# A product moved to GpSimd: the route's row multiplies the gate instead of the hidden tile in 16 units of an expert FFN

## The reference, cut to what matters

```python
masked_w = softmax over the 8 largest of x @ gate_w.T, 0 elsewhere   # tokens x 32
g = einsum('th,eih->tei', x, w_gate_proj)
u = einsum('th,eih->tei', x, w_up_proj)
h = silu(g) * u * masked_w[:, :, None]
out = einsum('tei,ehi->th', h, w_down_proj)
```

## Time and profile before

| | us |
|---|---|
| median of 3 runs | 777.99 |
| lowest, highest | 775.37, 778.99 |
| the profiled execution | 776.41 |
| its span | 774.6 |
| PE, DVE, ACT, POOL busy | 687.4, 548.6, 416.4, 247.1 |

### The profile page before, as it was taken

The page is one execution under the profiler, slowest core; times in us unless marked ns, Lnnn a source line. Parts: engine busy times, 40 slices in busy tenths (PEclk is TensorE's granted clock), DMA queues, the critical chain, the costliest instruction groups (busy, mean ns, idle before and its releaser), DMA issues.

```text
span 774.6 us, 10077 instructions
## 1 busy us (share of the span) xinstructions
PE 687.4 (89%) x3424; PEld 532.3 (69%) x3424; DVE 548.6 (71%) x1061; ACT 416.4 (54%) x814; POOL 247.1 (32%) x243
## 2 busy tenths in 40 slices
PE   5176746999998999999899999988899898999997
PEld 1154533455556788888788999977798776888885
DVE  5999997799998666565477666776766466544454
ACT  5575615646424544454667777766677445334342
POOL 0100001000053244454356565644465243212231
PEclk9598786999999999999999999999999999999999
DMA  7347753566664174443111111110112233433240
GB/s 238 118 151 236 231 166 113 149 209 199 202 165 149 51 205 137 142 164 120 45 41 46 37 43 41 41 42 15 42 55 76 82 123 111 127 118 100 84 137 27
DMA packets 43987, 88.67 MB, mean 114 GB/s; under 512 B 6136, under 2 KB 8448, under 8 KB 43936
## 3 DMA queue, kind: packets, MB, share of 16 engines
q1 hardware_dynamic: 43936, 88.04, 36.2%
HBM read 82.44 MB, written 5.57 MB: 114 GB/s over the span
## 4 chain that ended last, share of the span: by engine, by line
PE 57%; DVE 28%; issue 8%; ACT 6%; DMA 0%; DVEq 0%; POOL 0%; SPq 0%; ACTq 0%
PE bank L89 17%; PE bank L90 17%; PE bank L91 17%; DVE state L1115 9%; DVE read_out L1125 3%; PE bank L654 2%; DVE drive L1106 2%; ACT probs L967 2%; DVE bank L1268 1%; DVE u_sb L1028 1%; DVE scores L1388 1%; DVE stats L1035 1%; DVE x_norm L1048 1%; PE bank L485 1%; DVE head_out_lo L1017 1%
## 5 line engine op out<-in xcount | busy, mean ns | idle before, releaser
L1461 POOL TENSOR_TENSOR w_lo<-w_raw,w_hi 128x768 fp32r<-128x768 f32 (+1 forms) x90 | 152.1, 1690 | 290.9 <-ACT w_hi L737 289.6
L89 PE MATMUL bank<-xt_hi,w_hi 128*128 128x512 f32 x336 | 134.6, 401 | 0.0
L90 PE MATMUL bank<-xt_lo,w_hi 128*128 128x512 f32 x336 | 132.5, 394 | 0.0
L91 PE MATMUL bank<-xt_hi,w_lo 128*128 128x512 f32 x336 | 132.5, 394 | 0.0
L737 ACT ACTIVATE w_hi<-w_raw 128x768 fp32r<-128x768 f32 (+1 forms) x90 | 69.0, 766 | 87.4 <-PE bank L91 84.3
L1017 DVE TENSOR_TENSOR hidden_lo<-bank,hidden_hi 128x512 fp32r<-128x512 f32 x68 | 46.9, 689 | 55.2 <-ACT hidden_hi L737 55.1
L863 ACT ACTIVATE gated<-bank 128x512 f32<-128x512 f32 x84 | 50.3, 598 | 62.5 <-PE bank L485 42.9
L1275 DVE TENSOR_TENSOR bank<-gated,bank 128x512 f32<-128x512 f32 x64 | 44.5, 695 | 51.7 <-PE bank L91 51.0
L967 ACT ACTIVATE probs<-scores,row_min 128x256 f32<-128x256 f32 x128 | 63.9, 501 | 31.8 <-DVE row_min L1388 31.6
L412 PE MATMUL bank<-identity,read_out 128*128 128x128 f32 x272 | 40.9, 301 | 37.9 <-DVE read_out L1125 20.4
L412 PEld LDWEIGHTS bank<-identity,read_out 128*128 128x128 f32 x272 | 34.6, 155 | 57.3 <-DVE read_out L1125 31.3
(11 more groups left out here) (173 smaller groups left out, 1458.8 us busy)
## 6 DMA issues: line engine op xcount, KB each, us to landing
w_raw<-in_ffn_w SPq DMA_DIRECT2D x58, 384.0 KB, 3.2
b_rows<-bc_scratch SPq DMA_DIRECT2D x32, 256.0 KB, 3.7
c_rows<-bc_scratch SPq DMA_DIRECT2D x32, 256.0 KB, 3.6
w_raw<-fold_scratch SPq DMA_DIRECT2D x32, 256.0 KB, 2.6
route_bc<-route_scratch SPq DMA_DIRECT2D x32, 256.0 KB, 3.6
w_whole<-in_ffn_w SPq DMA_DIRECT2D x16, 384.0 KB, 4.5
route_bc<-route_scratch SPq DMA_DIRECT2D x32, 192.0 KB, 3.5
fold_scratch<-fold_sb SPq DMA_DIRECT2D x8, 512.0 KB, 4.7
```

The lines of the kernel that those rows point to most:

```text
L89: e.matmul(out, w_hi, m_hi, start=first, stop=False)
L90: e.matmul(out, w_hi, m_lo, start=False, stop=False)
L91: return e.matmul(out, w_lo, m_hi, start=False, stop=last)
L1461: e.tensor_tensor(lo[:, 0:n], w_raw[(p - WHOLE) % RAW][:, 0:n], hi[:, 0:n].bitcast(F32), ALU.subtract).then_inc(sem("w_lo"), 1)
```

## The change

The product with the route's row leaves VectorE in the plain units. GpSimd now multiplies `gated` by the row in place, as soon as ScalarE has written it and the row is there, and VectorE multiplies the result by the up bank straight into `hidden_whole`. GpSimd makes this product ahead of the weights that it splits in the same unit.

```diff
-        muls = [sum(routed[:u + 1]) for u in range(len(units))]
+        muls = [sum(routed[WHOLE:u + 1]) for u in range(len(units))]
...
                 if whole(u):
-                    e.tensor_tensor(h, g, h, ALU.mult).then_inc(sem("mul"), 1)
-                    at.wait_ge("mul", muls[u])
-                    at.wait_ge(f"ld_route{route_slot[u]}", route_landed[u])
+                    at.wait_ge("gate_routed", u + 1)
                     at.wait_ge("down", u - 2)
-                    e.tensor_tensor(hidden_whole[u % 3][:, :], h, route_bc[route_slot[u]][:, :],
-                                    ALU.mult).then_inc(sem("hid"), 1)
+                    e.tensor_tensor(hidden_whole[u % 3][:, :], g, h, ALU.mult).then_inc(sem("hid"), 1)
...
+            def route_gate(u):
+                at.wait_ge("silu", u + 1)
+                at.wait_ge(f"ld_route{route_slot[u]}", route_landed[u])
+                e.tensor_tensor(gated[u % 2][:, :], gated[u % 2][:, :], route_bc[route_slot[u]][:, :],
+                                ALU.mult).then_inc(sem("gate_routed"), 1)
+
             for u in range(U0):
                 n = u + 1
+                if whole(u):
+                    route_gate(u)
                 if u in split_in0:
                     rest_weights(split_in0[u])
```

## The result

The changed kernel takes 780.57 us (median of 20 runs, 777.95 to 783.76) against 777.64 of the kernel before in the same sessions (20 runs). The ratio is 1.0044, 95% interval 1.0027 to 1.0061: slower by 2.1 to 4.7 us. The forecast was 779.3 us, 1.3 us above its own before; the sign and the range hold, but the loss is larger than the sum gave: 2.9 us by the medians, 3.4 by the ratio.

What follows compares the result with a forecast made beforehand. TensorE was taken to set the unit, with its start waits and VectorE's late units counting. `x_norm` 1.3 us late gave 776.41 + 1.3 = 777.7 profiled; the median, 1.6 above, 779.3 us; range 776.0 to 783.4.

Steps and rivals of the forecast that it cites:

- TensorE's unit sets the middle: Middle plain units: TensorE goes on at 6.026 us a unit without waiting; VectorE's unit costs 6.01 us at most.
- The take of 0.96 us: Time VectorE loses when GpSimd's product arrives in its scan or drive: 0.96 us; 0.36 if it arrives during the read-out.
- rival 1: Plain units: the take is the whole 1.27 us, VectorE becomes the bound at 6.32 us a unit; median 783.3 us; 17%.
- Where the takes fall: Units 3 to 5: read-out or product, about 0.7, 0.4, 0.4 us; from unit 6 product, then scan: 0.6, 0.9, 0.96.
- the sign that I named: VectorE's drives in the new trace: some 2.15 us (1.20 + 0.96) in most units and none in the first.
- rival 2: Plain units: every GpSimd product falls into a read-out, taking 0.36 us; drives keep 1.20; median 777.1 us; 15%.
- The start: First units: first product 1.3 us later, scan pushed by 0.5, drive by 0.96; TensorE's wait at 146.41 grows by 2.7 us.
- T(1): Start of VectorE's unit 1, its first product: 146.27 us before, forecast at 149.0.
- rival 4: Behind TensorE's new 2.7 us wait at 146.5 its clock falls: +2.6 us more, median 781.9 us; 6%.
- the end: Last plain units up to `x_norm`: VectorE 2.0 us behind at unit 15, `x_norm` 1.3 us late, TensorE waiting 1.7 us.
- T(12): Start of VectorE's unit 12: 209.85 us before, forecast at about 212.3, 2.45 behind the old one.
- Rival 3: One collision more: a weight split takes its 1.57 us from scan or read-out; +2.9 us, median 780.9 us; 17%.

Runs made afterwards that it cites:

- e2: The changed kernel with GpSimd's product cut to 2 of the 512 columns, all waits kept; ratio to the kernel before 0.9957.
- e5: The changed kernel with GpSimd filling three tiles with zeros instead of multiplying the gate in the plain units; ratio to the kernel before 0.9980.
- e4: The changed kernel with TensorE making unit 3's gate product once more before it waits for the read-out in unit 2; ratio to the kernel before 1.0027.
- e10: The changed kernel once more, unaltered, for its trace; one run, 780.88 us.
- e3: The kernel before with one extra 128x512 GpSimd product in units 0 to 14, whose result nothing waits for; ratio to the kernel before 1.0068.

## Why the prediction was right in kind and short in size

**TensorE's unit sets the middle: right.** From 156.49 its units are 6.03 us without a wait up to unit 14, as forecast, and VectorE's unit of 5.05 + 0.97 = 6.02 follows it. Even e2, with VectorE's unit at 5.05, gained only TensorE's waits.

**The take of 0.96 us: right where it can be measured, and luck in the middle.** It can be measured where GpSimd's product had been waiting when VectorE's instruction ended: the drives at 144.44 and 155.57 lost 1.02 and 1.04 us, and no instruction lost the whole 1.27 to such a product. The Trainium skill, "SBUF — State Buffer", Terms, has the port held for the full instruction; these drives show some 0.2 us less, by records of GpSimd that the profile itself calls rough. Its section Who interferes with whom exempts a GpSimd instruction that only writes, and the scans and drives of e5 agree.

The 0.97 of the scans is no such measure. There GpSimd's product had already run 0.15 to 0.32 us beside the exempt one, and the scan lost what was left of it. And this settles by itself: if VectorE falls behind, more of GpSimd's product lies beside the exempt one and the scan loses less. The mean take is then what separates the two units, 6.03 - 5.05 = 0.98, within wide bounds of what the port costs. So a take of 1.27 need not have made VectorE the bound, as rival 1 has it (its sum is also 0.2 too high: 6.32 is 0.29 above 6.03, not 0.31), and the missing waits in the middle do not prove the 0.96. This is argued from the rows; no run has a longer take.

**Where the takes fall: right in the end, and against my own sign.** The product of unit 3 came in the scan of VectorE's unit 2 (153.48) and took from its drive, not from a read-out. From unit 3 on the arrival lay in the exempt product and the take in the scan behind it, as in my working. But the sign that I named was drives of some 2.15 us in most units and none in the first. It did not come: of the drives of units 0 to 11 only those of units 0 and 2 are long (2.22 and 2.23), and ten keep their 1.19. By the same list that spoke for rival 2, and it didn't hold either, as the scans were long instead.

**The start: right in its parts.** The first hidden tile is 1.4 us late behind the DMA (141.28 - 139.89), the second product takes 0.35 of the scan and the third 1.02 of the drive. T(1) is 2.1 late instead of 2.7, because the row's DMA landed 0.7 us sooner in this execution (139.89 - 133.35 = 6.5 us behind the read-out, 7.2 before).

**The step that failed: the clock, put at nothing in the sum and priced as rival 4.** I gave it 6% and argued that TensorE had kept full speed behind a wait of 2.27 us. There, it had worked 19 us without a pause (226.30 to 245.66). I had also put the whole new pause before the transposes, 3.5 us at 146.4. But TensorE also waits for the first hidden tile itself (0.33 us in the kernel before), so the pause came as two: waits of 2.06 and 2.13 us with 3.7 us of work between them (142.02 to 145.72). The fall cost 0.65 us in the transposes and 1.07 in gate and up, 1.7 us in the first trace, and 1.7 in the second (5.29 - 3.60). I had also held that VectorE alone would set the end. But once GpSimd's product sits in the scan, it arrives with TensorE's gate, so VectorE's units are tied to TensorE's, and what TensorE loses at the start moves T(12) as well: +3.7 instead of +2.45. e4 gives back 1.7 of it there, and 1.1 at `x_norm`. With 1.7 for the clock less 0.6 for the sooner DMA, my +1.3 becomes +2.4; of the rest, 0.3, the end has 0.2, where T(12) to T(15) took 20.9 us and not 20.7. Rival 3 had named the nearest number, 780.9, but its collision did not come: its price was 1.57, and the end is 0.2 longer than in my sum.

**Open.** That the clock fell, and that it did not without the second pause, is shown; which length of pause and which work around it let it fall is not, nor how often it falls. The interval of the ratio reaches from 2.1 to 4.7 us and tells neither 2.7 from 3.4 nor from more.

## What to carry to other kernels

Before an elementwise step is moved to GpSimd to relieve VectorE, look which engine sets the unit (with TensorE setting it, 11.7 us less on VectorE were worth about 4 where GpSimd's product was nearly free) and what VectorE does beside it: an instruction with two SBUF operands and GpSimd's take turns, while a product on a PSUM bank does not mind, so removing such a product also removes the room in which GpSimd was free. The first unit of a pipeline has no slack: keep the new hop out of it. And price a new pause of TensorE twice, once for itself and once for what the clock may do behind it: here that was 1.7 us.

## What was not expected of the hardware

The four `x_norm` instructions, with one SBUF operand tile each and small scalars beside it, take 1.37 us alone and 2.94 beside a weight split of GpSimd: one of the four then takes 1.97 us, the others their 0.41, so they take turns as well.

TensorE's clock fell to half behind two waits that lay close together (2.06 and 2.13 us in the first trace, 1.78 and 2.13 in e10), and also behind single ones of 3.41 (e3) and 3.17 us (e5). Waits of 2.27 (the kernel before), of 2.42 (e4, at 229.75) and of 1.77 and 0.41 (e4) left it at full speed. The router's wait of 3.37 us did either, so the length of a wait alone does not decide.
